# Two full-precision matmuls of a Mamba-2 scan, each issued as a pair of 64 stationary columns

## The chip, the cores and the metric

The kernel runs on one core of one Trainium2 chip. The metric is the device time of one execution in microseconds (us).

## The reference

One block of a Mamba-2 layer and a feed-forward layer with low-rank additions, both behind a layer norm and both added to the residual. The input is 2 sequences of 512 tokens with 512 channels. What the change touches is the state-space product (`_ssd`), which the reference writes over chunks of 32 tokens:

```python
scores = jnp.einsum('bcihn,bcjhn->bcijh', Cc, Bc) * Ldec * dtc[:, :, None, :, :]
y_intra = jnp.einsum('bcijh,bcjhp->bcihp', scores, xc)
states = jnp.einsum('bcjh,bcjhn,bcjhp->bchpn', dtc * dlast, Bc, xc)
...
y_inter = jnp.einsum('bcihn,bchpn->bcihp', Cc * jnp.exp(cum)[..., None], prev)
```

There are 128 heads of 64 channels in 8 groups of 16 heads, and a state of 128 values per channel. B and C are shared by the heads of a group. Behind it come a gate, a norm over each group and the output projection, then the feed-forward layer (1376 hidden channels).

## The kernel before, in words

Every engine has its own hand-written program, and semaphores tie the programs together. The order of the work on each engine is the order in which its program is written.

The kernel walks over the 8 groups, and in a group first runs `convolve`: 20 input projections (10 tiles of 128 channels by 2 sequences), each a product of 12 matmuls (L1237 to L1239, from the helper `split_product`), with the convolution behind them on VectorE and ScalarE. Then comes `scan` over 8 chunks of 128 tokens, 4 chunks for each sequence. The last group is followed by the feed-forward layer. The projections split their operands into a high and a low part of a faster type and add three products; the matmuls of the scan itself take plain 32-bit operands.

On TensorE a chunk c of the scan is this row of steps: `turn_x` of the next chunk (8 transposes, L1302), `match` of the next chunk, `inside` (16 heads, L1323), `across` (L1334, left out where a sequence begins), `new_state` (L1344, left out where a sequence ends), `project_out` of the chunk before (24 matmuls), `turn_g` (8 transposes, L1351) and `gate` of the next chunk (24 matmuls). In chunk 0 `inside` stands ahead of `turn_x`, half of the gate stands ahead of `new_state`, and there is no `across` and no `project_out`.

Two steps are touched. `match` multiplies B and C of a chunk (both with the 128 state values on the partitions) into `cbb[:, 0:P]`, a 128 by 128 tile in PSUM, and a transpose of B goes into the other half of that bank; there are 8 in a group, the first of them in the middle of `convolve`. `new_state` multiplies B (tokens on the partitions, `b_tok`) with the weighted x (`xw`), 128 by 1024 in two halves of 512, into the banks `xt[0]` and `xt[1]`; there are 6 in a group. VectorE waits for the first (`prepare_cb`) and for the second (`advance_state`), and reads all 128 partitions.

In the feed-forward layer `second_lora` (L1428) has matmuls with 16 rows of the array, and `low_product` has matmuls with 96 stationary columns.

Of the kernel before, what the change touches and what calls it, by code (L numbers as in the profile page):

```python
# [25 lines left out]
P = 128  # L26
# [97 lines left out]
def build(nc, x_in, wx_in, w_in, wdt_in, par_in, dt_bias_in, a_log_in, d_in,  # L124
# [5 lines left out]
    with ExitStack() as ctx:  # L130
        def sb(name, shape, dt=F32):
            return ctx.enter_context(nc.sbuf_tensor(name, shape, dt))
# [30 lines left out]
        bcT = sb("bcT", [P, 2, TOK])  # L163
# [8 lines left out]
        xw = sb("xw", [P, GCH])  # L172
        b_tok = sb("b_tok", [P, 2, P])
# [8 lines left out]
        def tok(c):  # L182
            return slice(c * P, (c + 1) * P)
# [44 lines left out]
        proj, xt, yb, cbb, ob = bank[0:2], bank[2:4], bank[4:6], bank[6], bank[7]  # L228
# [113 lines left out]
        def n_state(c):  # L342
            return sum(1 for q in range(c) if q % SEQ_CHUNKS < SEQ_CHUNKS - 1)
# [9 lines left out]
        def half(h):  # L353
            return slice(h * 512, (h + 1) * 512)
# [878 lines left out]
        def _(pe):  # L1233
# [71 lines left out]
            def match(g, c):  # L1305

                if c == 0:
                    pe.wait_ge(x_ready, g * HALVES + 2 * BATCH)
                else:
                    pe.wait_ge(b_tok_ready, g * CHUNKS + c)  # L1310
                pe.matmul(cbb[:, 0:P], bcT[:, 0, tok(c)], bcT[:, 1, tok(c)], start=True, stop=True)  # L1311
                pe.transpose(cbb[:, P:2 * P], bcT[:, 0, tok(c)], ident[:, :]).then_inc(cb_psum, 1)

            def inside(g, c):
# [22 lines left out]
            def new_state(g, c):  # L1337
                if c % SEQ_CHUNKS == SEQ_CHUNKS - 1:
                    return
                pe.wait_ge(b_tok_ready, g * CHUNKS + c + 1)  # L1340
                pe.wait_ge(xw_ready, g * NSTATE + n_state(c) + 1)
                pe.wait_ge(x_copied, g * CHUNKS + c + 2)
                for h in range(2):
                    last = pe.matmul(xt[h][:, :], b_tok[:, c % 2, :], xw[:, half(h)], start=True, stop=True)  # L1344
                last.then_inc(st_psum, 1)

            def turn_g(g, c):
# [23 lines left out]
            def convolve(g, first, beside=None):  # L1371
                for n in range(first, HALVES):
                    project_in(g, n)
                    if n == CB_AT:
                        match(g, 0)
                    if beside:
                        beside(n)
                gate(g, 0, (0,))
                turn_x(g, 0)
                gate(g, 0, (1,))  # L1380

            def scan(g, last):
                for c in range(CHUNKS):
                    if c == 0:
                        inside(g, c)
                    if c + 1 < CHUNKS:
                        turn_x(g, c + 1)
                        if last and c > 2:
                            pe.wait_ge(x_l_ready, CHUNKS + c - 2)
                        match(g, c + 1)  # L1390
                    if c > 0:
                        inside(g, c)
                        across(g, c)
                    if c == 0:
                        gate(g, 1, (0,))
                    new_state(g, c)
                    if c > 0:
                        project_out(g, c - 1)
                    if last and c > 1:
                        pe.wait_ge(b_tok_ready, g * CHUNKS + min(c + 2, CHUNKS))  # L1400
                        norm_transpose(1, c - 2)
                    turn_g(g, c)
                    if c + 1 < CHUNKS:
                        gate(g, c + 1, (0, 1) if c > 0 else (1,))
# [70 lines left out]
            def second(m, c):  # L1475
                r, s = rows_of(m), (2 * FT + m) % FSPLIT
                a, b = hid_h[0:r, m % FHID, tok(c)], hid_l[0:r, m % FHID, tok(c)]
                pe.matmul(bank[c][:, :], a, fw_h[0:r, s, :], start=(m == 0), stop=False)  # L1478
                pe.matmul(bank[c][:, :], a, fw_l[0:r, s, :], start=False, stop=False)  # L1479
                return pe.matmul(bank[c][:, :], b, fw_h[0:r, s, :], start=False, stop=(m == FT - 1))  # L1480

            for m in range(FT - FLATE):
                pe.wait_ge(hid_l_ready, m + 1)
                pe.wait_ge(w2_l_ready, m + 1)
                for c in (4, 5, 6, 7, 0, 2, 1, 3):
# [4 lines left out]
                    last = second(m, c)  # L1490
# [4 lines left out]
            for c in range(CHUNKS):  # L1495
                for m in range(FT - FLATE, FT):
                    last = second(m, c)
# [72 lines left out]
```

## Time and profile before

| | |
|---|---|
| median of 2 runs | 1971.91 us (1971.22 to 1972.60) |
| span of the profiled execution | 1972.3 us |
| TensorE busy | 1920.5 us (97% of the span) |
| TensorE loading stationary operands | 1562.7 us (79%) |
| VectorE, ScalarE, GpSimd busy | 1349.0, 1160.2, 599.1 us |
| mean granted clock of TensorE | 0.988 |

The profiled execution's span stands for its own time here; it lies between the two runs and within 0.4 us of the median. In the views, PE is TensorE's matmuls and PEld its loads of stationary operands, which run beside them. Each matmul with plain 32-bit operands leaves two records of each kind, one for each of its two passes, so the 96 matmuls of L1344 are 192 records and the 64 of L1311 are 128. A record of a matmul goes on after the next one has started, so the time that a matmul takes of the engine is read from start to start. In the shapes, `128*64` would be 128 rows by 64 columns of the array.

### The profile page before, as it was taken

The page shows a single profiled execution, that of the slowest core. Times are in us where ns is not written, and L with a number is a line of the kernel's source. Part 1 is how long each engine was busy: PE and PEld are TensorE (multiplying, and loading weights), DVE is VectorE, ACT ScalarE, POOL GpSimd, SP SyncE. Part 2 cuts the span into 40 slices and gives each one's busy share as a digit, 9 for nine tenths or more (in the row PEclk, how much of TensorE's full clock was granted, in tenths as well). Part 3 has the DMA queues.
Part 4 walks back from the last instruction along what each step waited for, and adds up shares of the span by engine and source line. Part 5 has one row for each costly group of instructions (what it writes and reads, how often), then busy time and mean ns, then how long its engine had stood idle before and what let it go on. Part 6 is the DMA issues. An engine that isn't in the chain of part 4 may idle for free. (4 is left out here: it accounts for less than half of the span.)

```text
span 1972.3 us, 30097 instructions
## 1 busy us (share of the span) xinstructions
PE 1920.5 (97%) x9642; PEld 1562.7 (79%) x9642; DVE 1349.0 (68%) x2342; ACT 1160.2 (59%) x2132; POOL 599.1 (30%) x553
## 2 busy tenths in 40 slices
PE   7789999999999999999999999999999999999999
PEld 5578887888878887888878878878788888877777
DVE  6787757776876768776777677776877688853112
ACT  5756665665766666666566565667666666642121
POOL 4431145112721163114411271116311452232221
PEclk9899999999999999999899999999999999999999
DMA  4321141214121222214121412122221421131101
GB/s 145 107 83 54 54 135 56 60 49 141 50 66 56 90 87 67 65 43 141 51 65 44 141 51 65 48 88 96 67 65 43 137 70 47 58 104 43 30 1 43
DMA packets 89940, 143.23 MB, mean 73 GB/s; under 512 B 20656, under 2 KB 23104, under 8 KB 89760
## 3 DMA queue, kind: packets, MB, share of 16 engines
q1 hardware_dynamic: 89760, 141.04, 23.2%
q8 instruction: 88, 1.44, 0.3%
q14 instruction: 92, 0.75, 0.1%
HBM read 136.28 MB, written 4.72 MB: 71 GB/s over the span
## 5 line engine op out<-in xcount | busy, mean ns | idle before, releaser
L1134 DVE SCALAR_TENSOR_TENSOR xdt<-bank,par,xdt 128x509 f32<-128x509 f32 (+2 forms) x480 | 326.4, 741 | 77.1 <-ACT xdt L736 75.9
L1237 PE MATMUL bank<-x_h,wx_h 128*128 128x512 f32 x648 | 257.0, 397 | 10.9 <-DVE xdt L1134 6.2
L574 POOL TENSOR_TENSOR skip<-skip,d_row 128x1024 f32<-128x1024 f32 x64 | 121.8, 1903 | 479.9 <-ACT skip L752 479.9
L1238 PE MATMUL bank<-x_l,wx_h 128*128 128x512 f32 x648 | 254.6, 393 | 0.0
L1323 PE MATMUL bank<-xdt,decay 128*128 128x64 f32 x2048 | 243.8, 279 | 10.8 <-issue 10.8
L1239 PE MATMUL bank<-x_h,wx_l 128*128 128x512 f32 x648 | 254.2, 392 | 0.0
L1323 PEld LDWEIGHTS bank<-xdt,decay 128*128 128x128 f32 x2048 | 241.8, 197 | 14.2 <-issue 13.3
L767 ACT ACTIVATE decay<-decay,cols 128x128 f32<-128x128 f32 x448 | 150.4, 396 | 124.1 <-DMA decay<-cum_scratch 122.5
L1237 PE MATMUL bank<-ow_h,gT_h 128*128 128x512 f32 x512 | 222.2, 434 | 0.0
L1237 PE MATMUL bank<-wg_h,x_h 128*128 128x512 f32 x512 | 207.4, 405 | 0.0
L1239 PE MATMUL bank<-wg_h,x_l 128*128 128x512 f32 x512 | 201.1, 393 | 0.0
L1238 PE MATMUL bank<-wg_l,x_h 128*128 128x512 f32 x512 | 201.0, 393 | 0.0
L1239 PE MATMUL bank<-ow_h,gT_l 128*128 128x512 f32 x512 | 200.0, 391 | 0.0
L1238 PE MATMUL bank<-ow_l,gT_h 128*128 128x512 f32 x512 | 199.4, 390 | 0.0
L736 ACT ACTIVATE xdt<-bank,par 128x512 f32<-128x512 f32 x160 | 124.3, 777 | 106.1 <-PE bank L1239 105.2
L1049 DVE TENSOR_TENSOR decay<-decay,cb 128x512 f32<-128x512 f32 x256 | 161.4, 692 | 10.7 <-ACT decay L775 10.7
L606 POOL TENSOR_TENSOR mean_sq<-ssq,eps 128x1 f32<-128x1 f32 x64 | 20.3, 317 | 465.1 <-ACT sg L829 465.1
L1237 PEld LDWEIGHTS bank<-x_h,wx_h 128*128 128x128 f32 x648 | 123.3, 190 | 37.1 <-issue 6.6
L557 POOL TENSOR_TENSOR wx_l<-raw,wx_h 128x512 fp32r<-128x512 f32 x81 | 105.9, 1308 | 132.5 <-ACT wx_h L666 132.5
L1014 DVE TENSOR_TENSOR xdt<-bank,cols 128x512 f32<-128x512 f32 x128 | 82.4, 685 | 89.9 <-PE bank L1302 89.9
L1239 PEld LDWEIGHTS bank<-x_h,wx_l 128*128 128x128 f32 x648 | 123.1, 190 | 26.1
L1070 DVE TENSOR_TENSOR y<-bank,skip 128x512 f32<-128x512 f32 x128 | 86.8, 688 | 83.2 <-PE bank L1323 83.1
(176 smaller groups left out, 3871.2 us busy)
## 6 DMA issues: line engine op xcount, KB each, us to landing
decay<-cum_scratch SPq DMA_DIRECT2D x256, 256.0 KB, 3.5
raw<-in_wx SPq DMA_DIRECT2D x80, 256.0 KB, 2.8
raw<-in_w SPq DMA_DIRECT2D x52, 256.0 KB, 2.8
skip<-in_w SPq DMA_DIRECT2D x32, 256.0 KB, 4.2
xw<-in_w SPq DMA_DIRECT2D x18, 256.0 KB, 4.5
state<-in_w SPq DMA_DIRECT2D x16, 256.0 KB, 2.7
sg<-in_w SPq DMA_DIRECT2D x16, 256.0 KB, 5.4
y<-in_w SPq DMA_DIRECT2D x16, 256.0 KB, 5.6
```

Source lines behind the costliest of these rows:

```text
L557: pool.tensor_tensor(wx_l[:, s, :], raw_x[:, s, :], wx_h[:, s, :].bitcast(F32), ALU.subtract).then_inc(wx_l_ready, 1)
L574: pool.tensor_tensor(s, s, spread(d_row[:, :], HDIM), ALU.mult).then_inc(skip_ready, 1)
L736: act.activation(conv[:, n % 4, :], conv_bank[n % 4][:, :], ACT.Identity, bias=par[:, CONV_B0 + t:CONV_B0 + t + 1], scale=par[:, t * TAPS ...
L767: last = act.activation(decay[:, h, :], decay[:, h, :], ACT.Relu, bias=cum_col(c, h))
L1014: last = dve.tensor_tensor(per_head(xdt[:, c % 2, half(h)]), per_head(xt[h][:, :]), spread(cols[:, DT, c, h * 8:h * 8 + 8], HDIM), ALU.mult)
L1049: dve.tensor_tensor(d, d, cb[:, c % 2, :].unsqueeze(1).broadcast_to([P, QH, P]), ALU.mult).then_inc(score_ready, 1)
L1070: last = dve.tensor_tensor(y[:, half(h)], yb[h][:, :], skip[:, c % 2, half(h)], ALU.add)
L1134: dve.scalar_tensor_tensor(out=conv[:, n % 4, s:], in0=conv_bank[n % 4][:, 0:SEQ - s], scalar=w, in1=conv[:, n % 4, s:], op0=ALU.mult, op1 ...
L1237: pe.matmul(dst, wh, xh, start=(k == 0), stop=False)
L1238: pe.matmul(dst, wh, xl, start=False, stop=False)
L1239: last = pe.matmul(dst, wl, xh, start=False, stop=(k == len(terms) - 1 and not more))
L1323: last = pe.matmul(yb[h // 8][:, (h % 8) * HDIM:(h % 8 + 1) * HDIM], decay[:, h, :], xdt[:, c % 2, h * HDIM:(h + 1) * HDIM], start=True, s ...
```

## The change

The matmul of `match` and both matmuls of `new_state` are each issued as two matmuls, one for stationary columns 0 to 63, written to PSUM partitions 0 to 63, and one for columns 64 to 127, written to partitions 64 to 127. The moving operand is the same for both, and all of it is streamed by each. The semaphore is raised by the last matmul of a step, as before. The numbers of instructions on the other engines, their order and all waits stay as they are.

```diff
-                pe.matmul(cbb[:, 0:P], bcT[:, 0, tok(c)], bcT[:, 1, tok(c)], start=True, stop=True)
+                for r in range(2):
+                    js = slice(c * P + r * 64, c * P + r * 64 + 64)
+                    pe.matmul(cbb[r * 64:r * 64 + 64, 0:P], bcT[:, 0, js], bcT[:, 1, tok(c)], start=True, stop=True)
                 pe.transpose(cbb[:, P:2 * P], bcT[:, 0, tok(c)], ident[:, :]).then_inc(cb_psum, 1)
...
                 for h in range(2):
-                    last = pe.matmul(xt[h][:, :], b_tok[:, c % 2, :], xw[:, half(h)], start=True, stop=True)
+                    for r in range(2):
+                        ns = slice(r * 64, r * 64 + 64)
+                        last = pe.matmul(xt[h][ns, :], b_tok[:, c % 2, ns], xw[:, half(h)], start=True, stop=True)
                 last.then_inc(st_psum, 1)
```

On TensorE, around `match` in chunk 1 of the scan (`bcT` holds B and C, `x_ch` is x, `decay` the scores, and `bank` any of the eight PSUM banks), the program was:

```order
L1239 MATMUL bank<-wg_h,x_l 128x512
L1302 MATMUL bank<-ident,x_ch 128x128 x8
L1311 MATMUL bank<-bcT 128x128
L1312 MATMUL bank<-ident,bcT 128x128
L1317 REGISTER_ALU
L1322 ISA
L1323 MATMUL bank<-xdt,decay 128x64 x4
```

and it now is:

```order
L1239 MATMUL bank<-wg_h,x_l 128x512
L1302 MATMUL bank<-ident,x_ch 128x128 x8
L1313 MATMUL bank<-bcT 64x128 x2
L1314 MATMUL bank<-ident,bcT 128x128
L1319 REGISTER_ALU
L1324 ISA
L1325 MATMUL bank<-xdt,decay 128x64 x4
```

Nothing moved; one matmul with an output of 128 by 128 became two of 64 by 128 at the same place, between transposes. On TensorE, around `new_state` in the same chunk, the program was:

```order
L1334 MATMUL bank<-state,bcT 128x512 x2
L1341 REGISTER_ALU
L1342 REGISTER_ALU
L1344 MATMUL bank<-xw,b_tok 128x512 x2
L1356 ISA
L1359 ISA
L1237 MATMUL bank<-ow_h,gT_h 128x512
```

and it now is:

```order
L1336 MATMUL bank<-state,bcT 128x512 x2
L1343 REGISTER_ALU
L1344 REGISTER_ALU
L1348 MATMUL bank<-xw,b_tok 64x512 x4
L1360 ISA
L1363 ISA
L1237 MATMUL bank<-ow_h,gT_h 128x512
```

Two matmuls became four of half the output partitions. The built instructions name a tile of the array of 128 rows by 64 columns, at column 0 and at column 64 in turn; those of before name the whole array.

## Rows read from the trace of the kernel before

**Rows 1.** Busy time of each engine; then TensorE and its granted clock in 40 slices.
```profile
PE 1920.5 (97%) x9642; PEld 1562.7 (79%) x9642; DVE 1349.0 (68%) x2342; ACT 1160.2 (59%) x2132; POOL 599.1 (30%) x553
...
PE   7789999999999999999999999999999999999999
...
PEclk9899999999999999999899999999999999999999
```

**Rows 2.** What TensorE waited for: us in total, times, longest.
```profile
PE bank L1247 <- DVE skip L944: 10.9, 7, 6.3
PE bank L1323 <- issue: 10.8, 6, 2.3
...
PE bank L1351 <- DVE y L1082: 3.8, 5, 0.8
```

**Rows 3.** TensorE's matmuls by line and shape: busy us, mean ns of one.
```profile
L1344 PE MATMUL bank<-xw,b_tok 128*128 128x512 f32 x192 | 90.7, 594 | 0.0
...
L1239 PE MATMUL bank<-x_h,wg_l 128*128 128x512 f32 x160 | 62.5, 391 | 0.0
...
L1311 PE MATMUL bank<-bcT 128*128 128x128 f32 x128 | 25.4, 281 | 0.0
...
L1239 PE MATMUL bank<-x_h,wg_l 128*96 128x512 f32 x24 | 9.4, 394 | 0.0
```

**Rows 4.** TensorE's matmuls in order of time around `new_state`: start us, us.
```profile
159.71 1.88 PE L1344 MATMUL bank<-xw,b_tok 128*128 128x512 f32 x4
161.03 0.80 PE L1237 MATMUL bank<-ow_h,gT_h 128*128 128x512 f32 x1
161.66 0.39 PE L1238 MATMUL bank<-ow_l,gT_h 128*128 128x512 f32 x1
161.89 0.39 PE L1239 MATMUL bank<-ow_h,gT_l 128*128 128x512 f32 x1
```

**Rows 5.** Its loads in the same stretch.
```profile
159.72 0.19 PEld L1344 LDWEIGHTS bank<-xw,b_tok 128*128 128x128 f32 x1 [0.24 <-issue]
160.15 0.19 PEld L1344 LDWEIGHTS bank<-xw,b_tok 128*128 128x128 f32 x1 [0.24 <-issue]
160.57 0.19 PEld L1344 LDWEIGHTS bank<-xw,b_tok 128*128 128x128 f32 x1 [0.24 <-issue]
```

**Rows 6.** Its matmuls in order of time around `match`.
```profile
154.09 0.39 PE L1311 MATMUL bank<-bcT 128*128 128x128 f32 x2
154.31 0.27 PE L1312 MATMUL bank<-ident,bcT 128*128 128x128 f32 x1
```

**Rows 7.** Its matmuls around one matmul with 16 rows of the array.
```profile
1854.88 0.40 PE L1446 MATMUL bank<-wx_h,gT_h 96*128 96x512 f32 x1
1855.12 0.40 PE L1446 MATMUL bank<-wx_l,gT_h 96*128 96x512 f32 x1
1855.44 1.12 PE L1428 MATMUL bank<-state,skip 16*128 16x512 f32 x2
1856.49 0.50 PE L1237 MATMUL bank<-x_h,wg_h 128*128 128x512 f32 x1
1856.83 0.39 PE L1238 MATMUL bank<-x_l,wg_h 128*128 128x512 f32 x1
```

**Rows 8.** The loads there, and the loads where 96 columns follow 16 rows.
```profile
1855.44 0.29 PEld L1428 LDWEIGHTS bank<-state,skip 16*128 16x128 f32 x2 [0.36 <-issue]
1856.49 0.19 PEld L1237 LDWEIGHTS bank<-x_h,wg_h 128*128 128x128 f32 x1 [0.76 <-issue]
1856.60 0.19 PEld L1238 LDWEIGHTS bank<-x_l,wg_h 128*128 128x128 f32 x1
...
1774.94 0.16 PEld L1237 LDWEIGHTS bank<-x_h,wg_h 128*96 128x96 f32 x1 [0.76 <-DVE x_l L950]
1775.02 0.16 PEld L1238 LDWEIGHTS bank<-x_l,wg_h 128*96 128x96 f32 x1
```

**Rows 9.** Stretches after two starts of a scan: us, busy us of each engine, granted clock.
```profile
332.00:339.00 7.00, 7.00 (x35) 6.81 (x35) 1.29 (x3) 0.00 (x0) 0.40 (x1) 0.53 0.48 151
...
967.00:978.00 11.00, 11.00 (x49) 10.42 (x49) 3.25 (x6) 1.97 (x6) 2.20 (x2) 0.53 0.31 96
```

## The prediction, made before the changed kernel ran

> **What bounds the kernel now.** The page's busy times come first: TensorE is busy for 97% of the span, VectorE for 68% and ScalarE for 59%, and the line of 40 slices shows TensorE at 9 everywhere after the first three [rows 1]. The view of its waits says how much of that is free to give: the largest entries are 10.9 us at the beginning of the kernel, 10.8 us at starts of a scan and 3.8 us ahead of `turn_g` [rows 2]. So in nearly all of the scan TensorE is the chain, and time added to it is time added to the end. The view by line and shape then gives the size of what is touched: 192 records at L1344 and 128 at L1311 [rows 3]. Since busy time counts each record's tail, I take the cost from the views in order of time, start to start.
>
> **What the touched work costs today.** The four records of a `new_state` begin at 159.71; the matmul behind them runs until L1238 starts at 161.66, and its own slot is 0.23 us (161.66 to 161.89), so the four end at 161.43 and hold the engine for 1.72 us, 0.43 us each [rows 4]. The loads start 0.43 us apart too, each just as a matmul starts, so they cost nothing of their own [rows 5]. In `match` the two records begin at 154.09 and the transpose behind them at 154.31, so a slot there is 0.11 us and the step is 0.22 us [rows 6]. In the whole kernel there are 48 of `new_state` and 64 of `match`.
>
> **Part 1: the halves of the array.** The slot of a matmul doesn't shrink with its stationary columns: those with 96 columns take 394 ns a record where those with 128 take 391 ns [rows 3]. Each 64-column matmul therefore still streams its 512 (or 128) columns in two passes, and there are eight slots of work in a `new_state` where there were four, and four in a `match` where there were two. What it costs depends on whether the left and the right half of the array can work at the same time. No row of before has two tiles side by side, so I bound it. If they never do, the extra is four slots, 4 x 0.43 = 1.72 us, and 2 x 0.11 = 0.22 us. If they do, the order of issue decides: left high pass, left low pass, right high pass, right low pass. The left low pass must wait for the left half to finish its high pass; the right high pass stands behind it and, if matmuls start in order, starts beside it; the right low pass starts beside the high pass of the next left one. For the eight matmul passes of `new_state` this makes five slots in place of four, for the four of `match` three in place of two. The extra is then 0.43 us and 0.11 us. The lower end is no extra at all: each half has four slots of its own work in a `new_state`, so four is the least in any order, and nothing here can give a gain. I take the side by side case with order kept, since the two matmuls share neither array columns nor output partitions; no row proves it.
>
> The Trainium skill says of this, in TensorEngine Tiling (Array Packing), Key Properties, that tiles "can execute LdWeights and Matmul in parallel". No row of before shows two tiles; by that rule the sum would be the one with five slots, without it the one with eight.
>
> **Part 2: entering and leaving the halves.** The trace has a near relative: `second_lora` uses 16 rows of the array between matmuls that use all. The slot of the matmul ahead is 0.24 us (1854.88 to 1855.12), so the array is free at 1855.35, yet the next load begins only at 1855.44, 0.09 us later, and is not hidden: of the two loads merged in that row the second ends at 1855.73 and lasted 0.18 us, so it began at 1855.55, which is when the first matmul streamed [rows 7, 8]. Leaving looks the same: two slots of 0.43 us end at 1856.41, the next load starts at 1856.49, and the one after it, which goes beside the matmul, at 1856.60 [rows 8]; L1238 at 1856.83 less a slot of 0.23 us gives 1856.60 as well [rows 7]. From 1855.35 to 1856.60 are 1.25 us for 0.86 us of work: 0.39 us for a visit. Inside 128-column work nothing like it is seen: loads overlap everywhere in [rows 5]. Of the 0.39 us, 0.17 us are waiting twice for the array to empty and 0.22 us two loads that lie open. A load that lies open is 0.11 us for 128 columns (1856.49 to 1856.60) and 0.08 us for 96 (1774.94 to 1775.02) [rows 8], so by its columns 0.055 us for 64. A visit of the changed kernel has one of 64 and one of 128, so it should cost 0.39 - 0.055 = 0.34 us. The bounds: nothing, if a split by columns is not treated like one by rows, and 0.40 us. I take 0.34, because the row is of the same kind, a matmul on part of the array between two on all of it.
>
> The Trainium skill (the same page and section) says that changing the tiling mode, and not just the tile, drains TensorE, and it makes no difference between rows and columns; by that rule the bound of nothing falls away. The rows show the drain for rows alone.
>
> **Part 3: what else moves.** The loads: twice as many, each of half the columns, in slots of 0.43 us where a load starts at once; no cost in `new_state`. In `match` a slot is 0.11 us, and a 64-column load of 0.055 us fits into it. The semaphores are raised by the last matmul of a step, so VectorE's `prepare_cb` and `advance_state` are released later by what the step has grown; VectorE has a third of its time free. Cover is to be had in one place: in chunk 0 TensorE waits ahead of `turn_g` for VectorE's y, which doesn't depend on `new_state`; that is 3.8 us in five places, at most 0.8 us each [rows 2], and a `new_state` that ends 0.77 us later eats into it. I credit 3.8 us. The waits at starts of a scan come after a chain that begins with TensorE's own work, so they shift and hide nothing.
>
> **The sum.** `new_state`: (0.43 + 0.34) x 48 = 37.0 us. `match`: (0.11 + 0.34) x 64 = 28.8 us. Together 65.8 us, less 3.8 us of cover, is 62 us on a span of 1972.3 us: 2034 us, 3.1% slower. The span is 0.4 us over the median of the two runs, which doesn't matter here. With a visit at 0.20 us this case gives (0.63 x 48) + (0.31 x 64) - 3.8 = 46 us, or 2018; with a visit of 0.40 us and a right half whose loads come a little late, about 2050.
>
> **The rivals.**
> - *The halves work one after the other, with the visit's cost.* `new_state` (1.72 + 0.34) x 48 = 98.9 us, `match` (0.22 + 0.34) x 64 = 35.8 us, less 3.8 us: 131 us, 2103. For it: the passes of a 32-bit matmul come in pairs, and nothing in the trace shows two matmuls streaming at once. Against it: nothing that the two would share, except the moving operand, which is read twice.
> - *The change does not split the array.* The chip runs 64-column matmuls on the whole array, as it does those with 96 columns, which come at 394 ns with no extra [rows 3]. Then there is no visit and no overlap: 1.72 x 48 + 0.22 x 64 = 96.6 us, less 3.8 us: 2065. The tiles named in the instructions speak against it.
> - *The halves overlap, and entering costs nothing.* 0.43 x 48 + 0.11 x 64 = 27.7 us, less some 2.5 us of cover: 1997, within 2%. For it: both tiles span all rows, and loads beside matmuls on the same rows are the rule here [rows 5]; the drain seen is with fewer rows. It decides the sign of "slower by 2%" at a visit of about 0.14 us.
> - *Not slower.* The engine lets the right half's high pass start beside the left half's high pass, by looking past the waiting low pass, and there is no drain. Four slots stay four, two stay two, and the time is 1972. It would need both, and the starts of before are strictly in the order of the program.
> - *No load runs beside a matmul on the same rows.* Then the halves also go one after the other, and each load of 0.055 us but the first lies open: 7 x 0.055 x 48 + 3 x 0.055 x 64 = 29 us on top of 131: 2132. Rows 5 speak against it: loads of all 128 rows start 0.01 us behind the start of a matmul on the same rows and cost nothing [rows 5]. A rule of the Trainium skill points that way: TensorE: Matmul & The Clock Gate, in Part 3, The mechanism, says that a load overlaps with matmuls in flight only where the row group differs, and a split by columns leaves both tiles on all rows. The trace disagrees for the whole array.
> - *The clock.* After two starts of a scan the granted clock was about half for 7 and for 10 to 11 us, behind a wait of TensorE [rows 9]. If the new pauses let it fall at five more starts, for some 10 us at half each, 25 us come on top: 2059.
>
> **How the numbers follow.** About 2% (39 us, so 2011) is what a measurement of this kernel can tell from no change. Forecast with five slots and a visit of 0.34 us: 0.45. One after the other with visit: 0.18. No split: 0.10. Overlap without visit: 0.12. Not slower: 0.05. Loads in the open: 0.03. Clock: 0.07. Slower by over 2% is 0.45 + 0.18 + 0.10 + 0.03 + 0.07 = 0.83, less 0.01 that I keep for faster, by something not thought of: 0.82. Within 2% is 0.12 + 0.05 = 0.17. The range must take in the overlap without visit (1997) below and the serial halves (2103) above: 1994 to 2106. That leaves out the case of not slower and that of open loads, 0.08, and the edges.
>
> **What would show it.** In the trace of the changed kernel L1348 should have 384 records of 128*64 and L1313 256. In one `new_state` the eight records should start in pairs, one slot of 0.43 us apart, and the stretch from the first to the matmul behind should be about 2.5 us, against 1.72 us; `match` with its surroundings should take about 0.67 us in place of 0.22 us. If the starts are all 0.43 us apart, the halves run one after the other; if no gap of about 0.09 us with an open load stands ahead of the first and behind the last, there is no price for the visit. I am wrong altogether if TensorE's waits, now a few us, grow into tens, or if the clock's slices at 8 become many.

## The result, and the profile after

The changed kernel took 1992.86 us (median of two runs, 1991.22 to 1994.49) against 1971.91 us: 1.15% slower, with a 95% interval of 0.74% to 1.56%. Run again in more rounds, with a smaller spread, it was 1.24% slower (1.06% to 1.43%), which is 24 us. The forecast was 2034 us, 3.1% slower, with a range from 1994 us. The first measurement lies 1 us below the range, the second (1996.59 us) 3 us inside it; either way the loss is little over a third of what was forecast.

The page of the changed kernel, with the lines that answer to [rows 1]; the column of each slice is busy share or clock in tenths:

```profile
span 1992.7 us, 30737 instructions
...
PE 1947.9 (98%) x9962; PEld 1536.6 (77%) x9962; DVE 1349.1 (68%) x2342; ACT 1158.8 (58%) x2132; POOL 598.4 (30%) x553
...
PE   7799999999999999999999999999999999999999
...
PEclk9899999999999999999999999999999999999999
```

TensorE is the bound as before and has 320 more records. The clock has one low slice fewer than before (the second of the two in [rows 1]); what that is worth is told under waits and clock. What it waited for, against [rows 2]:

```profile
PE bank L1325 <- issue: 8.0, 6, 1.6
...
PE bank L1355 <- DVE y L1082: 1.8, 6, 0.3
```

By line and shape, against [rows 3], the records have doubled and name half of the array, so the chip does split it:

```profile
L1348 PE MATMUL bank<-xw,b_tok 128*64 128x512 f32 x384 | 93.0, 605 | 0.0
...
L1313 PE MATMUL bank<-bcT 128*64 128x128 f32 x256 | 28.6, 303 | 0.0
```

Twice the records of `new_state`, each as long as before, cover 93.0 us where they covered 90.7 us. At 0.43 us a slot, 384 of them one after the other would take 165 us, so two must run at a time. The matmuls in order of time, at the `new_state` that [rows 4] show for before:

```profile
158.48 1.45 PE L1336 MATMUL bank<-state,bcT 128*128 128x512 f32 x3
159.87 1.94 PE L1348 MATMUL bank<-xw,b_tok 128*64 128x512 f32 x8
161.73 0.50 PE L1237 MATMUL bank<-ow_h,gT_h 128*128 128x512 f32 x1
162.07 0.39 PE L1238 MATMUL bank<-ow_l,gT_h 128*128 128x512 f32 x1
```

and its loads, against [rows 5]:

```profile
159.86 0.20 PEld L1348 LDWEIGHTS bank<-xw,b_tok 128*64 128x64 f32 x4 [0.76 <-issue]
160.35 0.14 PEld L1348 LDWEIGHTS bank<-xw,b_tok 128*64 128x64 f32 x2 [0.29 <-issue]
160.78 0.14 PEld L1348 LDWEIGHTS bank<-xw,b_tok 128*64 128x64 f32 x2 [0.28 <-issue]
161.73 0.19 PEld L1237 LDWEIGHTS bank<-ow_h,gT_h 128*128 128x128 f32 x1 [0.81 <-issue]
161.84 0.19 PEld L1238 LDWEIGHTS bank<-ow_l,gT_h 128*128 128x128 f32 x1
```

The loads come in four pairs. The first row holds two of them: one pair in the open at 159.86, and one at 159.92 (the row's end less the 0.14 us of a load), when the first matmuls stream. The others start at 160.35 and 160.78, each 0.43 us behind the last. From 159.92 four slots end at 161.64, and 0.09 us later the next step's load starts: eight passes in four slots, not in five. What the step has grown by stands at its two ends. The last three of the four records of `across` begin at 158.48, so the array is free at 158.48 + 3 x 0.43 = 159.77. The next load starts at 159.86, and the first load after it that runs beside a matmul of the whole array at 161.84. From 159.77 to 161.84 are 2.07 us for 1.72 us of work: 0.35 us for the visit (with a fifth slot the forecast had about 2.5 us here). `match`, against [rows 6]:

```profile
153.41 0.60 PE L1302 MATMUL bank<-ident,x_ch 128*128 128x128 f32 x4
153.94 0.44 PE L1313 MATMUL bank<-bcT 128*64 128x128 f32 x4
154.31 0.33 PE L1314 MATMUL bank<-ident,bcT 128*128 128x128 f32 x1
154.48 0.33 PE L1325 MATMUL bank<-xdt,decay 128*128 128x64 f32 x2
```

The transposes end their slots at 153.41 + 4 x 0.11 = 153.85, and `inside` starts at 154.48: 0.63 us. In the kernel before, the trace has 0.33 us from `match` at 154.09 to `inside` at 154.42. That is 0.30 us more. There is no third slot in it: from the start of the step at 153.94 to the transpose at 154.31 are 0.37 us, which an open load of 0.055 us, two slots of 0.11 us and a gap of 0.09 us fill. So the 0.30 us are the visit.

### The profile page after: what moved, and what is told of

Its sections match the earlier page's. It is cut to its first block, busy times and chain, and to the rows that moved or that the text cites. A ratio compares the mean times of both kernels' runs of the same rounds, so it can differ in the third digit from the quotient of the medians.

```text
span 1992.7 us, 30737 instructions
## 1 busy us (share of the span) xinstructions
PE 1947.9 (98%) x9962; PEld 1536.6 (77%) x9962; DVE 1349.1 (68%) x2342; ACT 1158.8 (58%) x2132; POOL 598.4 (30%) x553
## 4 chain that ended last, share of the span: by engine, by line
PE 93%; DVE 4%; ACT 2%; issue 1%; DMA 0%; SPq 0%; DVEq 0%; ACTq 0%
PE bank L1237 21%; PE bank L1239 20%; PE bank L1238 20%; PE bank L1325 12%; PE bank L1336 4%; PE bank L1348 4%; PE bank L1302 3%; PE bank L1355 3%; PE bank L1313 1%; PE bank L1482 1%; PE bank L1483 1%; PE bank L1484 1%; DVE y L1082 1%; PE bank L1314 1%; DVE xdt L1134 1%
## 5 line engine op out<-in xcount | busy, mean ns | idle before, releaser
L1325 PE MATMUL bank<-xdt,decay 128*128 128x64 f32 x2048 | 239.2, 276 | 8.0 <-issue 8.0
L1237 PE MATMUL bank<-ow_h,gT_h 128*128 128x512 f32 x512 | 210.9, 412 | 0.0
L1238 PEld LDWEIGHTS bank<-x_l,wx_h 128*128 128x128 f32 x648 | 123.2, 190 | 25.0
```

The costliest lines, as they stand in the source:

```text
L1237: pe.matmul(dst, wh, xh, start=(k == 0), stop=False)
L1238: pe.matmul(dst, wh, xl, start=False, stop=False)
L1325: last = pe.matmul(yb[h // 8][:, (h % 8) * HDIM:(h % 8 + 1) * HDIM], decay[:, h, :], xdt[:, c % 2, h * HDIM:(h + 1) * HDIM], start=True, s ...
```

## The experiments

All of them stand against the kernel before, run beside them on the same chip; ratios are with their 95% intervals.

**One step at a time.** Only the split of `new_state` is kept:

```diff
                 for h in range(2):
-                    last = pe.matmul(xt[h][:, :], b_tok[:, c % 2, :], xw[:, half(h)], start=True, stop=True)
+                    for r in range(2):
+                        ns = slice(r * 64, r * 64 + 64)
+                        last = pe.matmul(xt[h][ns, :], b_tok[:, c % 2, ns], xw[:, half(h)], start=True, stop=True)
```

> Only new_state is split. Theory A (the two halves of the array work fully side by side, four slots stay four, and a visit to the split array costs 0.35 us, as the changed kernel's trace reads at one place): 48 x 0.35 = 17 us, less 2 to 3 us where TensorE waits ahead of turn_g in chunk 0: about +14 us, 1986. Rival B (there is a fifth slot after all and 15 us of it were given back by a kinder clock): 48 x (0.43 + 0.35) = 37 us, 2007. Rival C (the whole cost is in match, where the neighbours are short transposes): no change, 1972.

Measured: 0.65% slower (0.45% to 0.85%), 12.8 us. And only the split of `match`:

```diff
-                pe.matmul(cbb[:, 0:P], bcT[:, 0, tok(c)], bcT[:, 1, tok(c)], start=True, stop=True)
+                for r in range(2):
+                    js = slice(c * P + r * 64, c * P + r * 64 + 64)
+                    pe.matmul(cbb[r * 64:r * 64 + 64, 0:P], bcT[:, 0, js], bcT[:, 1, tok(c)], start=True, stop=True)
```

> Only match is split. Theory A: 64 visits of about 0.30 us (0.55 of a drain twice and two open loads, of which the one for the transpose is read as 0.055 us) = 19 us, less what TensorE's waits at starts of a scan and ahead of across absorb (up to 5 us): +14 to +19 us, 1986 to 1991; with the split of new_state alone it adds up to more than the +21 us measured for both, and the difference is cover or clock. Rival B (short steps are hidden by the queue): under +5 us. Rival C (the halves go one after the other in short matmuls): 64 x 0.5 = 32 us, 2004.

Measured: 0.66% slower (0.42% to 0.91%), 13.0 us. Both are a little under A's figure, and their sum, 1.3%, agrees with the 1.24% of both together. A fifth slot would have cost `new_state` 37 us, and serial halves `match` 32 us, before a few us of cover; both fall. A third slot in `match` (7 us more) is ruled out by the rows above rather than by this time, whose interval reaches 18 us.

**The same half twice.** Is the overlap real, and does a matmul on half of the array take full time? Both 64-column matmuls of `new_state` use the left half (the state's upper 64 rows are not computed):

```diff
                 for h in range(2):
-                    last = pe.matmul(xt[h][:, :], b_tok[:, c % 2, :], xw[:, half(h)], start=True, stop=True)
+                    for r in range(2):
+                        last = pe.matmul(xt[h][0:64, :], b_tok[:, c % 2, 0:64], xw[:, half(h)], start=True, stop=True)
```

> new_state is split, but both 64-column matmuls use columns 0 to 63 of B and the left half of the array (so the state's upper 64 rows are not computed). Theory A (the gain of two halves is that they work side by side, and a 64-column matmul takes as long as one of 128 columns): eight slots in place of four, 48 x (1.72 + 0.35) = 99 us, less some 3 us that TensorE's waits in chunk 0 absorb: about +95 us, 2065. Rival B (a matmul on half of the array takes half the time): no more than the +13 us of the split alone, 1982.

Measured: 4.96% slower (4.62% to 5.30%), 98 us, against 99 less 3. The same step in order of time takes twice as long for the same eight records:

```profile
162.14 3.65 PE L1345 MATMUL bank<-xw,b_tok 128*64 128x512 f32 x8
```

So a 64-column matmul holds its half for a whole slot, and the other half's work is free only because it is the other half's.

**All left, then all right.** In what order do the halves start? `new_state` has its loops swapped:

```diff
-                for h in range(2):
-                    for r in range(2):
-                        ns = slice(r * 64, r * 64 + 64)
+                for r in range(2):
+                    ns = slice(r * 64, r * 64 + 64)
+                    for h in range(2):
                         last = pe.matmul(xt[h][ns, :], b_tok[:, c % 2, ns], xw[:, half(h)], start=True, stop=True)
```

> Both steps are split as in the change, but new_state issues both matmuls of columns 0 to 63 (the two halves of xw) and then both of columns 64 to 127. Theory A (TensorE starts the matmuls of each half of the array when that half is free, whatever stands between in the program): still four slots in a new_state, the same time as the changed kernel, 1993. Rival B (starts are strictly in program order, and the built program has the passes of neighbouring 64-column matmuls interleaved): the right half starts beside the last left pass, seven slots: 3 x 0.43 x 48 = 62 us more, 2055. Rival C (a short look-ahead of one matmul only): five to six slots, 2013 to 2034.

Measured: 1.15% slower (0.86% to 1.45%), 1992.28 us, the same as the change. The step in order of time is as long as in the change, 1.94 us:

```profile
160.76 1.94 PE L1348 MATMUL bank<-xw,b_tok 128*64 128x512 f32 x8
```

In the view by windows (busy us and count of matmuls, then of loads), the 0.03 us in which the step begins already hold two matmuls and two loads:

```profile
160.75:160.78 0.03, 0.02 (x2) 0.02 (x2) 1.00 0.50 137
```

Two passes of the same half can't be meant, since those stand 0.43 us apart in the run before. So though four left passes stand ahead of the first right one in the program, it starts with the first of them; starts in the order of the program would have taken seven slots, 3.0 us. The rule on which the forecast counted a fifth slot, starts in the order of the program, doesn't hold between the halves.

**How far ahead.** `inside` has 32 passes a chunk for each half and so can show where this ends. First it is split in the plain way, with `new_state` and `match` as before:

```diff
-                    last = pe.matmul(yb[h // 8][:, (h % 8) * HDIM:(h % 8 + 1) * HDIM], decay[:, h, :],
-                                     xdt[:, c % 2, h * HDIM:(h + 1) * HDIM], start=True, stop=True)
+                    for r in range(2):
+                        ts = slice(r * 64, r * 64 + 64)
+                        last = pe.matmul(yb[h // 8][ts, (h % 8) * HDIM:(h % 8 + 1) * HDIM], decay[:, h, ts],
+                                         xdt[:, c % 2, h * HDIM:(h + 1) * HDIM], start=True, stop=True)
```

> Only inside (16 heads, stationary decay of 128 columns, 64 moving columns) is split in the same way; new_state and match are as before. Its passes are 0.111 us apart today, which is the load of 128 columns, while 64 moving columns need about 0.055 us. Theory A (loads of both halves run together, as the starts 6 ns apart in the changed kernel's new_state say): a pair of passes takes about 0.056 us, so 32 x 0.055 = 1.8 us less for each of 64 chunks, 113 us less, plus 64 visits of 0.35 us = 22 us: about 1881. Rival B (the sequencer can't issue four instructions in 0.056 us): half the gain or none, 1930 to 1994. Rival C (loads of the halves go one after the other when they are dense): no gain and a visit, 1994.

Measured: 1896.35 us, 3.76% faster (3.49% to 4.03%), 74 us, between A's 88 and B's 40 at the most. The step in the order of time, in the kernel before and then with the split:

```profile
118.84 3.68 PE L1323 MATMUL bank<-xdt,decay 128*128 128x64 f32 x32
```

```profile
153.66 2.08 PE L1325 MATMUL bank<-xdt,decay 128*64 128x64 f32 x64
```

Twice the records in little over half the time. A stretch of 0.3 us in the step shows the same in the view by windows (the counts take in records still running when it begins), the split first and the kernel before second:

```profile
154.90:155.20 0.30, 0.30 (x18) 0.30 (x15) 1.00 0.00 0
```

```profile
155.00:155.30 0.30, 0.30 (x5) 0.30 (x4) 1.00 0.00 0
```

The passes of `inside` stood 0.11 us apart for the load of 128 columns; two loads of 64 columns run together and let a pair of passes through in 0.058 us (32 pairs and the tail of the last record, 0.22 us, make the 2.08 us). This is the one of the three steps where the split has something to win: the others stream as many columns as they did. An estimate from the rows: 64 steps of 32 x (0.111 - 0.058) us are 108 us less, and 64 visits of 0.35 us are 22 us more: 86 us, close to A's figure. What it lacks is in new waits; TensorE now reaches `across` before ScalarE has the gate ready:

```profile
PE bank L1336 <- ACT sg L783: 19.8, 16, 1.9
```

where the same wait was 2.8 us in the kernel before. With two smaller waits that grew (ahead of `new_state` and of `turn_g`) and one that shrank, TensorE waits some 22 us more. That leaves 64 us; a higher granted clock, told below, gives 9 more, 73 us in all. Then the order within a quarter of four heads is changed, left heads first:

```diff
-                for h in range(GH):
-                    if h % QH == 0:
-                        pe.wait_ge(score_ready, (g * CHUNKS + c) * QUARTERS + h // QH + 1)
...
+                for q in range(QUARTERS):
+                    pe.wait_ge(score_ready, (g * CHUNKS + c) * QUARTERS + q + 1)
+                    for r in range(2):
+                        ts = slice(r * 64, r * 64 + 64)
+                        for h in range(q * QH, (q + 1) * QH):
+                            last = pe.matmul(yb[h // 8][ts, (h % 8) * HDIM:(h % 8 + 1) * HDIM], decay[:, h, ts],
+                                             xdt[:, c % 2, h * HDIM:(h + 1) * HDIM], start=True, stop=True)
+                    last.then_inc(y_psum, 1)
```

> inside is split as in the run with inside alone (-3.8%), but within a quarter of 4 heads the left half's four matmuls come first and then the right half's four. Between the first left and the first right pass stand 8 passes and their loads. Theory A (each half of the array has its own queue, filled ahead): the same time, 1896. Rival B (the look-ahead holds only the two matmuls that the change and the left-first run needed): the halves work mostly one after the other, inside takes 3.5 us again and the visit comes on top, 1985 to 1995. Something between (a queue of four passes a half): 1930 to 1960.

Measured: 1918.93 us, 2.69% faster (2.37% to 3.01%), between A's time and the middle case. And all 16 left heads come ahead of all 16 right ones:

```diff
-                for h in range(GH):
-                    if h % QH == 0:
-                        pe.wait_ge(score_ready, (g * CHUNKS + c) * QUARTERS + h // QH + 1)
...
+                for r in range(2):
+                    ts = slice(r * 64, r * 64 + 64)
+                    for h in range(GH):
+                        if r == 0 and h % QH == 0:
+                            pe.wait_ge(score_ready, (g * CHUNKS + c) * QUARTERS + h // QH + 1)
+                        last = pe.matmul(yb[h // 8][ts, (h % 8) * HDIM:(h % 8 + 1) * HDIM], decay[:, h, ts],
+                                         xdt[:, c % 2, h * HDIM:(h + 1) * HDIM], start=True, stop=True)
+                        if r == 1 and h % QH == QH - 1:
+                            last.then_inc(y_psum, 1)
```

> inside is split, and all 16 left matmuls (32 passes) come before the 16 right ones; VectorE is told of each quarter by the right ones. Theory A with a queue of 32 passes or more a half: starts of both halves still side by side, about 1896 to 1905 (VectorE hears of the first quarters a little later). Theory A with a shorter queue: the right half starts only when the left half is nearly through, up to 3.5 us again for a step: 1950 to 1995. This run is to read the depth of the look-ahead from the trace.

Measured: 1979.42 us, 0.43% slower (0.28% to 0.58%), within the shorter queue's range: nothing of the gain is left. The step in the two runs, quarters first:

```profile
154.46 2.69 PE L1325 MATMUL bank<-xdt,decay 128*64 128x64 f32 x64
```

```profile
154.52 3.77 PE L1325 MATMUL bank<-xdt,decay 128*64 128x64 f32 x64
```

The same 64 passes take 2.08, 2.69 or 3.77 us, by their order alone. In the last run two stretches of 0.3 us, before and after the middle of the step, hold half the records of the plain split:

```profile
155.30:155.60 0.30, 0.30 (x9) 0.30 (x7) 1.00 0.00 0
...
156.60:156.90 0.30, 0.30 (x9) 0.30 (x8) 1.00 0.00 0
```

So one half works and the other idles. Only around 156.3 do the counts rise (9 records in 0.1 us, against 5 or 6), for some 0.3 us: there the last left and the first right passes overlap. With one half at work a pass takes 0.058 us, where a pass of 128 stationary columns took 0.111 us for the same 64 moving ones, so the load sets the pace. The halves run ahead of each other by a few passes and no more: 4 left passes ahead of a right one cost nothing (the run with loops swapped), 8 cost over a third of what the step had gained (0.61 of 1.60 us), 32 all of it. The passes of the swapped loops are 0.43 us long and those of `inside` 0.058 us, so the three runs don't fix one depth. Theory A stands with a short queue; its long one falls.

**Is the price for a visit or for a matmul?** `across` and `new_state` are split as well as `inside`, with which they stand side by side:

```diff
-                    last = pe.matmul(proj[h][:, :], bcT[:, 1, tok(c)], state[:, half(h)], start=True, stop=True)
+                    for r in range(2):
+                        cs = slice(c * P + r * 64, c * P + r * 64 + 64)
+                        last = pe.matmul(proj[h][r * 64:r * 64 + 64, :], bcT[:, 1, cs], state[:, half(h)], start=True, stop=True)
```

> inside, across and new_state are split, match is not. In chunks 1 to 7 of a group the three stand side by side, in chunk 0 inside and new_state stand apart. Theory A (the price is for a visit to the split array, not for a split matmul): one visit for all three where inside alone already had one, so only the 8 new_states of chunk 0 add a visit, 8 x 0.35 = 3 us: 1896 + 3 = 1899, although 192 more matmuls are split than in the run with inside alone. Rival B (each split step costs what new_state cost alone, +13 us for 48 visits): 1896 + 13 for new_state + 13 for across = 1922.

Measured: 1897.31 us, 3.85% faster (3.57% to 4.13%), within noise the same as the 3.76% with `inside` alone (on another chip, each against the kernel before beside it). B's 26 us more lie outside the intervals, A's 3 us inside. The split of `new_state`, which cost 12.8 us by itself, costs next to nothing where its neighbours are split. The timeline has no gap between the steps, 1.72 us from start to start, as many as the four slots need:

```profile
153.91 1.89 PE L1338 MATMUL bank<-state,bcT 128*64 128x512 f32 x8
155.63 1.89 PE L1350 MATMUL bank<-xw,b_tok 128*64 128x512 f32 x8
```

Last, `match` joins them, with the transpose of B put ahead of it:

```diff
-                for r in range(2):
-                    js = slice(c * P + r * 64, c * P + r * 64 + 64)
-                    pe.matmul(cbb[r * 64:r * 64 + 64, 0:P], bcT[:, 0, js], bcT[:, 1, tok(c)], start=True, stop=True)
-                pe.transpose(cbb[:, P:2 * P], bcT[:, 0, tok(c)], ident[:, :]).then_inc(cb_psum, 1)
+                pe.transpose(cbb[:, P:2 * P], bcT[:, 0, tok(c)], ident[:, :])
+                for r in range(2):
+                    js = slice(c * P + r * 64, c * P + r * 64 + 64)
+                    last = pe.matmul(cbb[r * 64:r * 64 + 64, 0:P], bcT[:, 0, js], bcT[:, 1, tok(c)], start=True, stop=True)
+                last.then_inc(cb_psum, 1)
```

> All four plain 32-bit steps are split, and in match the transpose comes first, so that in chunks 1 to 7 the split product of match, inside, across and new_state make one visit. In chunk 0 the three steps stand apart, and the match of chunk 0 stands alone in the convolution. Theory A (the price is for a visit): 56 + 3 x 8 + 8 = 88 visits in place of 64 of inside alone, 24 x 0.3 = 7 us more: 1896 + 7 = 1903, less what waits take back. Rival B (each split match costs the +13 us for 64 that it cost alone): 1897 + 13 = 1910.

Measured: 1899.85 us, 3.63% faster (3.47% to 3.79%). That is 0.2% behind the run with three steps, some 4 us. A's 7 us were counted from `inside` alone; from the run with three steps, 72 visits, it is 16 visits more, 5 us, and B has 13. The difference of the two ratios has an interval from 2 us less to 11 us more, so A fits and B doesn't. Each of the versions with `inside` split in pairs beats both kernels.

**Waits and clock.** The visits read from the trace add up to 48 x 0.35 + 64 x 0.30 = 36 us, and the kernel lost 21 to 24 us. Where are the rest? Two more profiles were taken, of the changed kernel and of the one before.

> The changed kernel once more, in more rounds, to narrow the interval (1.0074 to 1.0156) and to have a second profile. If the 35.7 us of visits (48 x 0.35 + 64 x 0.295) are the cost and TensorE's waits at starts of a scan, ahead of turn_g and ahead of across take back about 7 us every time, the time without any help of the clock would be +28 us, 1.4%; if the clock helps every time as in the first profile (granted 0.992 against 0.988), +21 us, 1.05%. The split of one step each gave +0.65% and +0.66%, which would add up to 1.3%.

> The kernel before once more, for a second profile: if the granted clock of its first one, 0.988, was chance, this one lies elsewhere between 0.986 and 0.993; if it belongs to the kernel, it is 0.988 again, with the same three starts of a scan at half clock.

Measured: a span of 1994.7 us at a granted clock of 0.990, against 1969.6 us at 0.989. The first pair was 1992.7 us at 0.992 against 1972.3 us at 0.988. A clock of 0.988 over 1972.3 us is 23.7 us lost at the lower level, so in the first pair the clock helped the changed kernel by 23.7 - 15.9 = 7.8 us, in the second by 21.7 - 19.9 = 1.8 us. Without it the pairs agree: 20.4 + 7.8 = 28.2 us and 25.1 + 1.8 = 26.9 us.

Every execution has its span and clock on record, and span times clock (an estimate of the span at full clock, as if the stretches at the lower level were full of work) scatters far less than the span: in the 17 executions of the kernel before beside the first experiments, by 5 us where the span scatters by 19 us, at clocks from 0.984 to 0.994. The means of this product tell what a change costs apart from the clock:

| run | span against before | at full clock | clock, before and run |
|---|---|---|---|
| `new_state` alone | +12.1 us | +12.4 us | 0.990, 0.990 |
| `match` alone | +14.1 us | +11.6 us | 0.990, 0.989 |
| the change, second measurement | +24.2 us | +26.3 us | 0.990, 0.991 |
| the change with loops swapped | +23.0 us | +26.3 us | 0.990, 0.992 |
| the same half twice | +96.2 us | +92.1 us | 0.989, 0.987 |
| `inside` in pairs | -74.0 us | -65.2 us | 0.990, 0.994 |
| `inside`, left first in a quarter | -52.6 us | -40.7 us | 0.989, 0.995 |
| `inside`, all left first | +8.5 us | +19.4 us | 0.989, 0.994 |
| three steps | -75.1 us | -62.9 us | 0.989, 0.995 |
| all four | -71.8 us | -60.8 us | 0.990, 0.995 |

So the clock gave the change 2 us in the mean, and most of the 7.8 us of the first pair were chance. But with `inside` split it lay higher in the mean of every run (0.992 to 0.996 in 29 executions), which was worth 9 to 12 us each, for `inside` in pairs 9 of its 74 us. Why it does is not shown. At full clock the run with all left heads first is 19 us slower than the kernel before, about its 64 visits.

The other 8 us of the change are waits that TensorE had anyway and that a later arrival shortens, in both pairs: at starts of a scan, ahead of `turn_g` and ahead of `across`. For the second pair, the kernel before first:

```profile
PE bank L1323 <- issue: 9.8, 6, 2.4
...
PE bank L1351 <- DVE y L1082: 3.8, 5, 0.8
...
PE bank L1334 <- ACT sg L783: 2.8, 8, 0.4
```

```profile
PE bank L1325 <- issue: 6.9, 6, 1.6
...
PE bank L1355 <- DVE y L1082: 1.5, 5, 0.3
```

The third of them is gone or too small for the list. Together they give back 2.9 + 2.3 + up to 2.8, some 8 us, and 36 - 8 = 28 us.

## Why the prediction was wrong

- **TensorE bounds the kernel, and what is added to it is added to the end.** Right, but the cover was put at 3.8 us and was about 8 us. The prediction said that the waits at starts of a scan shift and hide nothing. They fell from 10.8 to 8.0 us in the first pair and from 9.8 to 6.9 us in the second.
- **Part 1, the slots: the step that failed.** The prediction had the right half's high pass stand behind the left half's low pass, "if matmuls start in order", and so counted five slots for four and three for two: 0.43 x 48 + 0.11 x 64 = 27.7 us of the 62. The runs showed no extra slot. The pairs start together from the first pass, with two left passes ahead (the change) and with four (the swapped loops); order cost time only in the runs with 8 and 32 ahead. The evidence given for order, that the records of before start in the order of the program, came from a kernel in which no two tiles stand side by side; it said nothing on two halves. The case that came true was priced as half of the rival "not slower", at 0.05, because it was tied to a free visit. Four slots with a paid visit would have been 0.34 x 112 - 3.8 = 34 us, 2006, and belonged among the rivals.
- **What makes up the difference.** Of the 62 us forecast, 27.7 us are the slots that didn't come, 2 us the cheaper visits (36 us in place of 38), 4 us the larger cover and 2 to 8 us the clock. That leaves 20 to 26 us, against 21 to 24 us measured.
- **The rival that came nearest** in time, overlap without a visit at 1997, was wrong on both counts: the visit is paid and the slots aren't. Its time is near by luck, 27.7 us of slots in place of about 28 us of visits net of waits.
- **That the halves work side by side at all, and that a 64-column matmul keeps its slot.** Right: the same half twice cost 98 us (91 to 104), against 95 expected.
- **Part 2, the visit.** Right to the size: 0.34 us taken from the matmuls with 16 rows of the array [rows 7, 8], 0.35 us measured at `new_state`, 0.30 us at `match`. With three steps side by side it is paid once. By the Trainium skill, TensorEngine Tiling (Array Packing), Key Properties, a change of the tiling mode drains TensorE and a change of tile doesn't; these runs agree for columns, at 0.09 us from the end of the last slot to the next load, with loads in the open behind.
- **Loads in the open** (a rival at 0.03). It fell. Loads of both column halves, on all rows, run beside matmuls at no cost, two at a time: in `new_state` every pair but the first. TensorE: Matmul & The Clock Gate, Part 3, The mechanism, of the Trainium skill says in its list that a load overlaps matmuls in flight only where the row group differs; taken by itself, that doesn't hold here. The same section also lets a load go ahead into a background weight buffer, which these rows don't contradict.
- **The clock** (a rival at 0.07, against the change). The first profile after the change has one low slice of the clock fewer than before, not more, and over the second measurement's executions the clock gave the change 2 us. The granted clock of one and the same kernel went from 0.984 to 0.994, about 20 us of its time.

What stays open: why the order by quarters costs 0.61 us a step. If a half could have about four passes waiting, the step would take some 36 slots of 0.058 us, 0.2 us more than in pairs (an estimate); it takes about 43. The exact depth was not measured. Open too is why the clock is higher with `inside` split.

## What to carry to other kernels

In this kernel, splitting a full 128-column matmul by columns won only where the load of the stationary operand set the pace, as it did with 64 moving columns (`inside`); with 128 (`match`) or 512 (`new_state`) it won nothing and paid some 0.3 us for each visit. So split neighbours together, put the two halves next to each other in the program, and look first for a step whose passes are as far apart as its loads are long.

## What the runs showed of the hardware

- Two matmuls on the two column halves start within 0.02 us of each other though two to four passes stand between them in the program; with 8 or 32 between them a step of 64 passes grew from 2.08 to 2.69 and 3.77 us.
- Two loads of 64 columns run together: the passes of `inside` went from 0.11 us each to 0.058 us a pair, in a step that fell from 3.68 to 2.08 us.
- The price of a visit is about the same for a split by columns (0.35 us) as the rows showed for one by rows (0.39 us, less the shorter load).
